# One decoder layer on one core: two steps at a time in every other period of the first attention

## The chip, the cores and the metric

The kernel runs on one core of a Trainium2 chip, in one launch. The metric is the device time of a launch in microseconds (us). The core has five engines that run side by side and wait for each other by semaphores only: TensorE (PE, with its weight loads PEld), VectorE (DVE), ScalarE (ACT), GpSimd (POOL) and SyncE (SP), which issues the DMAs. Each engine takes its own instructions in the order in which the program lists them.

## The reference, cut to what matters

```python
def attn(x, emb_weight, qkv_w, o_w):          # first attention: B 4, S 512, C 256, 16 heads of 64
    q, k, v = split_heads(x @ qkv_w.T)
    bias = emb_weight[rel_buckets(S)].transpose(2, 0, 1)[None]
    scores = einsum('bhqd,bhkd->bhqk', q, k) * 64 ** -0.5 + bias
    a = einsum('bhqk,bhkd->bhqd', softmax(scores), v)
    return merge_heads(a) @ o_w.T
x = layernorm(x + attn(x, ...))
x = layernorm(x + attn2(x, ctx, ...))         # 16 heads of 16: causal self part plus a context part
x = layernorm(experts(x, ...))                # 3 of 8 zones for each of the 4 sequences
```

Only the first attention is changed.

## The kernel before

`attention_1` works through 32 units. A unit u is a pair of heads (u % 8) of one sequence (u // 8). A software pipeline of 36 slots (`for t in range(SLOTS)`), each of four periods (`for i in range(NT)`), spreads a unit over five slots. In slot t these units are at work at the same time:

- unit t: projections. `proj_qk(t, 0)` (queries) and `proj_qk(t, 1)` (keys) are six float16 matmuls of 512 columns each (L409), `proj_v` 24 of 128 columns (L419). All three write `bank_a`. ACT (`evacuate` L610, `store_v` L616) and DVE (`low` L742) take the result out as a high and a low half in float16.
- unit t - 1: `maximum`, in each period two matmuls on half of the rows (L432) into `bank_m`, and on DVE two custom passes (L753) that give the row maximum of each of two heads for 128 queries, in `mx`.
- unit t - 2: `rows` in period 0: four transposes in float32 (L441) turn `mx` into rows of `bank_a`; ACT copies them twice with a scale into the two heads of `q2` (L623) and counts `act_rows`. Then the scores: in each period two (one for each head) of 128 keys by 512 queries, two matmuls each (L454, L455), into `bank_s[0]` and `bank_s[1]`. DVE adds the near bias (`add_bias` L762), ACT takes the exponential (L635). Scores 0 to 5 of a unit stand in periods 1, 2, 3 of slot u + 2, scores 6 and 7 in period 0 of slot u + 3. A score waits for the exponential of the score two before it, since it takes that bank.
- units t - 2 and t - 3: `pv` (L464), in each period the product of 128 keys with the values for both heads, in float32, two matmuls of 64 output rows (four records), added up in `bank_o` over four periods. POOL adds the exponentials up (`add_exponentials` L844) and makes a low half of the sums (L849). ACT and DVE take `bank_o` out in period 2 (`high_o` L648, `low_o` L767).
- unit t - 4: `sums` (L482) in period 0 turns the sums into a column of `bank_e[0]`, DVE inverts them (`invert` L774), and in each period `project_out` (L504) makes 128 tokens of the output product, three pairs of matmuls of 256 columns, one bank for each head. DVE adds the first head to `x_acc` (`add_out` L784), ACT scales the second (`weigh` L656), POOL adds that (L856).

The order on PE within a period is: first score, projection, second score, (period 0: `rows`, `sums`), `maximum`, `project_out`, `pv`. ACT and DVE follow the same order with their parts; in period 0 ACT does both exponentials, then the copies of `rows`, then `weigh`.

The waits that matter around the change are in `proj_qk`, for i == 0, and in `score`, for j == 0:

```python
if u > 1:
    pe.wait_ge(sm["act_rows"], 2 * u - 2)     # proj_qk(u, 0): bank_a is free of the rows of unit u - 2
...
    pe.wait_ge(sm["act_rows"], 2 * u + 2)     # score(u, 0): its own rows of maxima are in q2
```

`proj_qk(u, 1)` waits for `low` of the queries and `proj_v(u)` for `low` of the keys (`dve_a`), since all of them use `bank_a`.

Of the kernel before, what the change touches and what calls it, by code (L numbers as in the profile page):

```python
# [11 lines left out]
P = 128  # L12
# [197 lines left out]
def attention_1(nc, io, x_acc, xhi, xlo, ident, second, lines32, lines16, far_lines, halves2):  # L210
# [6 lines left out]
    with ExitStack() as ctx:  # L217
# [3 lines left out]
        def bank(n):  # L221
# [5 lines left out]
                                       "pool_lo pe_sum dve_r pe_o act_o dve_o pe_e0 pe_e1 dve_x act_x pool_x "  # L227
                                       "cst2 w2_in w2_hi w2_lo ld_ctx bias pe_br act_br dve_br dve_e1 dve_lo")
        moved = [sm[f"moved{c}"] for c in range(3)]
# [14 lines left out]
        junk = [sb(f"junk{p}", [P, S], F16) for p in range(2)]  # L244
        mx = [sb(f"mx{p}", [P, NT, 2]) for p in range(2)]
        pt = sb("pt", [P, RING, S])
        ps = [sb(f"ps{h}", [P, S]) for h in range(2)]
# [29 lines left out]
        def out_banks(u, qb):  # L277

            return bank_s if u >= LAST and qb % 2 == 1 else bank_e

# [9 lines left out]
        def sync(sp):  # L290
# [33 lines left out]
            for c in range(3):  # L324
                sp.dma_start(k2[c][D1:ROWS1, :, :], io["select1"]).then_inc(sm["cst"], DMA)
            for b in range(1, B):
                load_x(b)
                load_w(2 * b)
                load_w(2 * b + 1)
# [12 lines left out]
            for u in range(UNITS):  # L342
# [23 lines left out]
                if u == 4:  # L366
                    for dst, name in ((second.tri_q[:, :, :], "tri_q"), (second.identm[:, :, :], "identm"),
                                      (second.ident16[:, :], "ident16"), (second.braw[:, :], "b2")):
# [15 lines left out]
        def tensor(pe):  # L384
# [50 lines left out]
            def rows(u):  # L435
                pe.wait_ge(sm["dve_b"], 8 * u + 8)
                pe.wait_ge(sm["act_v"], min(u + 2, UNITS))
                if u == UNITS - 1:
                    pe.wait_ge(sm["act_rows"], 2 * u)
                for qb in range(NT):  # L440
                    mm = pe.transpose(bank_a[0:2, qb * P:(qb + 1) * P], mx[u % 2][:, qb, :], ident[:, :])  # L441
                mm.then_inc(sm["pe_rows"], 1)
# [25 lines left out]
            def sums(u):  # L468
                if u < UNITS - 1:
                    pe.wait_ge(sm["pool_lo"], 2 * u + 2)  # L470
                else:
                    pe.wait_ge(sm["dve_lo"], 2)
                if u == 0:
                    pe.wait_ge(sm["ones"], 1)
                    turned.done(pe)
                else:
                    pe.wait_ge(sm["dve_x"], 4 * u if u <= LAST else 4 * u - 1)
                for h in range(2):
                    for qb in range(NT):
                        for i in range(2):  # L480
                            n = h * NT + qb
                            mm = pe.matmul(bank_e[0][:, n:n + 1], psh[h][:, i, qb * P:(qb + 1) * P], ones[:, :], start=i == 0,  # L482
                                           stop=i == 1)
                mm.then_inc(sm["pe_sum"], 1)

            def project_out(u, qb):
                n = 4 * u + qb
                if qb == 0:
                    pe.wait_ge(sm["dve_o"], u + 1)
# [3 lines left out]
                if n == 4 * LAST + 1:  # L493
                    pe.wait_ge(sm["act_s"], 8 * UNITS)
                elif n > 4 * LAST + 1:
                    pe.wait_ge(sm["dve_e1"], n - 1 - 4 * LAST)
                elif n > 0:
                    pe.wait_ge(sm["dve_x"], n)
                    pe.wait_ge(sm["act_x"], n)
                tok = slice(qb * P, (qb + 1) * P)  # L500
                for n, (i, w) in enumerate(((0, wohi), (0, wolo), (1, wohi))):
                    for h in range(2):
                        hd = slice(h * D1, (h + 1) * D1)
                        mm = pe.matmul(out_banks(u, qb)[h][:, 0:C], a16[u % 2][hd, i, tok], w[hd, u % PAIRS, :], start=n == 0,  # L504
                                       stop=n == 2)
                        if n == 2:
                            mm.then_inc(sm[f"pe_e{h}"], 1)
# [29 lines left out]
            for t in range(SLOTS):  # L537
                for i in range(NT):
# [18 lines left out]
                    if 0 <= t - 1 < UNITS:  # L557
                        maximum(t - 1, i)
                    if 0 <= t - 4 < UNITS:
                        project_out(t - 4, i)  # L560
                    u = t - 2 if i > 1 else t - 3
                    if 0 <= u < UNITS:
                        pv(u, (i + 2) % 4)
                    for e in bridge_at(t, i):
                        bridge(e)

        def scalar(act):
# [82 lines left out]
            def weigh(u, qb):  # L650
                n = 4 * u + qb
                act.wait_ge(sm["pe_e1"], n + 1)
# [3 lines left out]
                act.activation(part[n % 4][:, :], bank_e[1][:, 0:C], ACT.Identity, scale=r[u % 2][:, 1, qb:qb + 1]  # L656
                               ).then_inc(sm["act_x"], 1)
# [39 lines left out]
        def vector(dve):  # L697
# [46 lines left out]
            def maximum(u, qb):  # L744
                if qb == 0 and u > 1:
                    dve.wait_ge(sm["pe_rows"], u - 1)
                if qb == 0:
                    dve.wait_ge(sm[f"rt{u % 3}"], DMA * (u // 3 + 1))
                for h in range(2):
# [26 lines left out]
            def add_out(u, qb):  # L776
                dve.wait_ge(sm["pe_e0"], 4 * u + qb + 1)
# [6 lines left out]
                dve.scalar_tensor_tensor(x_acc[:, o:o + C], out_banks(u, qb)[0][:, 0:C], r[u % 2][:, 0, qb:qb + 1], x_acc[:, o:o + C],  # L784
                                         ALU.mult, ALU.add).then_inc(sm["dve_x"], 1)
                if u >= LAST:
                    dve.wait_ge(sm["pe_e1"], 4 * u + qb + 1)
                    dve.wait_ge(sm["dve_x"], 4 * u + qb + 1)
                    dve.scalar_tensor_tensor(x_acc[:, o:o + C], out_banks(u, qb)[1][:, 0:C], r[u % 2][:, 1, qb:qb + 1], x_acc[:, o:o + C],
                                             ALU.mult, ALU.add).then_inc(sm["dve_e1"], 1)  # L790

            for t in range(SLOTS):
                for i in range(NT):
                    u = t - 2 if i > 0 else t - 3
                    if i == 2 and 0 <= t - 3 < UNITS:
                        low_o(t - 3)
# [16 lines left out]
                    if 0 <= t - 1 < UNITS:  # L813
                        maximum(t - 1, i)
                    if 0 <= t - 4 < UNITS:
                        add_out(t - 4, i)
                    if t in (6, 10) and i == 1:
                        split_w2(t // 10)
                    if t == 11 and i == 1:
                        dve.wait_ge(sm["cst2"], 4 * DMA)  # L820
                        dve.tensor_scalar(second.bias[:, :], second.braw[:, :], WS, None, ALU.mult).then_inc(sm["bias"], 1)
# [11 lines left out]
        def gpsimd(pool):  # L833
# [1162 lines left out]
```

## Time and profile before

| | |
|---|---|
| runs | 1284.3 us median of 3 (1284.05 to 1286.31) |
| profiled execution | 1287.09 us, of which 1285.4 us span |
| PE busy | 1183.4 us (92% of the span) |
| DVE busy | 924.5 us (72%) |
| ACT busy | 820.9 us (64%) |
| POOL busy | 498.6 us (39%) |
| granted TensorE clock, mean | 0.981 |

The profile is of one execution. Engine times are busy times; a PE record overlaps the next one, because matmuls are pipelined, so that the distance between two starts says what a matmul costs the queue. The first attention takes the span from the start to about 568 us. The chain of work that ended last runs over PE for 75% of the span, DVE 14%, ACT 4%.

### The profile page before, as it was taken

The numbers are of one execution on the slowest core, as the hardware profiler recorded it, in microseconds if no ns is written. First come the engines' busy times: TensorE is split into PE (matmuls) and PEld (weight loads), VectorE is DVE, ScalarE is ACT, GpSimd is POOL, SyncE is SP. The second block draws the span as 40 slices with busy tenths as digits, with TensorE's granted clock in tenths as the row PEclk, the third lists the DMA queues.
The fourth block names the chain that finished last, engine by engine and source line by source line (L and its number), as shares of the span: only waits on it lengthen the run. The fifth ranks groups of instructions, "written<-read, shape, count | busy, mean of one in ns | idle before, by whom it ended". The sixth has DMA issues, their size and how long they took to land.

```text
span 1285.4 us, 25128 instructions
## 1 busy us (share of the span) xinstructions
PE 1183.4 (92%) x8870; PEld 542.9 (42%) x8870; DVE 924.5 (72%) x2376; ACT 820.9 (64%) x1577; POOL 498.6 (39%) x519
## 2 busy tenths in 40 slices
PE   6799999999999999868899988888888999999998
PEld 2344444444444444334333233322332366666666
DVE  3777777777777777767788787778876567656564
ACT  3566666666666666634677766676666777667663
POOL 0167878888777778914212111131111131000000
PEclk9999999999999999988999999999999899999999
DMA  7634333322233332021121221122100523232300
GB/s 221 172 98 117 96 93 84 111 80 80 80 84 83 84 82 81 13 71 42 46 81 43 65 61 42 43 56 69 42 26 1 197 89 109 75 139 97 118 17 17
DMA packets 82483, 103.00 MB, mean 80 GB/s; under 512 B 12627, under 2 KB 74067, under 8 KB 82327
## 3 DMA queue, kind: packets, MB, share of 16 engines
q1 hardware_dynamic: 81174, 100.87, 26.8%
q8 instruction: 71, 1.16, 0.4%
q10 hardware_dynamic: 160, 0.39, 0.1%
q14 instruction: 54, 0.43, 0.1%
q0 software_dynamic: 1024, 0.13, 0.1%
HBM read 65.37 MB, written 10.68 MB: 59 GB/s over the span
## 4 chain that ended last, share of the span: by engine, by line
PE 75%; DVE 14%; ACT 4%; issue 4%; DMA 1%; POOL 1%; ACTq 0%; SPq 0%; DVEq 0%; POOLq 0%
PE a_s L1299 10%; PE a_o L464 9%; DVE a_mx L1607 8%; PE a_m L1285 7%; PE a_o L1218 6%; PE a_a L409 6%; PE a_s L454 5%; PE a_s L455 4%; PE a_m L1173 4%; PE a_e L504 3%; PE a_a L419 3%; PE a_m L432 3%; PE a_a L166 3%; PE a_s L1200 3%; PE a_s L1285 2%
## 5 line engine op out<-in xcount | busy, mean ns | idle before, releaser
L1607 DVE TENSOR_REDUCE a_mx<-a_m 128x1 f32<-128x512 f32 (+3 forms) x512 | 271.5, 583 | 80.4 <-PE a_m L1173 71.3
L1432 ACT ACTIVATE a_pt<-a_s 128x512 f32<-128x512 f32 (+3 forms) x512 | 235.0, 515 | 115.4 <-PE a_s L1200 112.9
L635 ACT ACTIVATE a_pt<-a_s 128x512 f32<-128x512 f32 x256 | 149.5, 597 | 167.4 <-DVE a_s L762 139.6
L753 DVE CUSTOM_DVE_ANT_0 a_junk<-a_m,a_rtile 128x512 f16<-128x512 f32 x256 | 167.3, 687 | 0.7 <-issue 0.7
L844 POOL TENSOR_TENSOR a_ps<-a_ps,a_pt 128x512 f32<-128x512 f32 x128 | 159.8, 1271 | 0.7 <-ACT a_pt L635 0.7
L464 PE MATMUL a_o<-a_pt,a_v 128*64 128x512 f32 x512 | 139.8, 624 | 2.6 <-DVE a_a L767 2.5
L1853 POOL TENSOR_SCALAR_AFFINE_SELECT a_pt<-a_pt 128x512 f32<-128x512 f32 x64 | 40.6, 635 | 229.4 <-ACT a_pt L1432 229.4
L762 DVE TENSOR_TENSOR a_s<-a_s,a_near 128x218 f32<-128x218 f32 (+1 forms) x256 | 107.9, 433 | 13.8 <-PE a_s L455 10.6
L454 PE MATMUL a_s<-a_q,a_k 128*128 128x512 f16 x256 | 99.3, 388 | 7.1 <-ACT a_pt L635 6.1
L742 DVE TENSOR_TENSOR a_nat<-a_a,a_nat 128x512 f16<-128x512 f32 x64 | 44.3, 692 | 84.2 <-ACT a_nat L610 84.2
L844 POOL TENSOR_TENSOR a_ps<-a_pt 128x512 f32<-128x512 f32 x64 | 80.1, 1273 | 57.0 <-ACT a_pt L635 57.0
L1173 PE MATMUL a_m<-a_qk 48*128 48x512 f16 (+3 forms) x320 | 78.4, 349 | 23.0 <-DVE a_mx L1607 22.6
L856 POOL TENSOR_TENSOR x_acc<-x_acc,a_part 128x256 f32<-128x256 f32 x120 | 87.2, 726 | 32.1 <-DVE x_acc L784 31.4
L455 PE MATMUL a_s<-a_q,a_k 74*128 74x512 f16 x256 | 98.2, 383 | 0.0
L849 POOL TENSOR_TENSOR a_psh<-a_ps,a_psh 128x512 f16<-128x512 f32 x62 | 70.5, 1157 | 68.0 <-ACT a_psh L641 67.9
L1218 PE MATMUL a_o<-a_pt,a_vy 128*17 128x512 f32 (+3 forms) x768 | 86.6, 523 | 0.0
L1734 DVE SCALAR_TENSOR_TENSOR x_acc<-a_s,a_wbc,x_acc 128x256 f32<-128x256 f32 x48 | 23.2, 484 | 85.8 <-PE a_s L1299 85.6
L454 PEld LDWEIGHTS a_s<-a_q,a_k 128*128 128x128 f16 x256 | 24.8, 97 | 131.1 <-issue 70.5
L1496 ACT ACTIVATE a_held<-a_m 128x512 f32<-128x512 f32 x72 | 43.0, 597 | 57.9 <-PE a_m L1285 57.1
L1200 PE MATMUL a_s<-a_qk 49*128 49x512 f16 (+3 forms) x320 | 70.4, 342 | 2.0 <-ACT a_pt L1432 1.9
L1173 PEld LDWEIGHTS a_m<-a_qk 48*128 48x128 f16 x320 | 22.4, 93 | 113.9 <-DVE a_mx L1607 86.4
L504 PE MATMUL a_e<-a_wohi,a_a 64*128 64x256 f16 x496 | 61.7, 271 | 5.3 <-issue 4.6
(295 smaller groups left out, 2622.8 us busy)
## 6 DMA issues: line engine op xcount, KB each, us to landing
a_rtile<-lines SPq DMA_DIRECT2D x32, 448.0 KB, 3.9
a_q<-a_nat SPq DMA_DIRECT2D x192, 64.0 KB
a_k<-a_nat SPq DMA_DIRECT2D x192, 64.0 KB
a_vy<-in_Wa SPq DMA_DIRECT2D x12, 1024.0 KB, 4.9
a_vy<-in_Wb SPq DMA_DIRECT2D x12, 1024.0 KB, 7.4
a_qk<-halves SPq DMA_DIRECT2D x40, 128.0 KB, 2.7
halves<-a_held SPq DMA_DIRECT2D x16, 256.0 KB, 2.3
halves<-a_held SPq DMA_DIRECT2D x32, 128.0 KB, 2.4
```

The source lines that it names most:

```text
L454: pe.matmul(bank_s[h][:, :], k1[c][:, h, ks], q1[c][:, h, ::-1], start=True, stop=False)
L455: pe.matmul(bank_s[h][:, :], k2[c][:, h, ks], q2[c][:, h, ::-1], start=False, stop=True).then_inc(sm["pe_s"], 1)
L464: mm = pe.matmul(bank_o[h * D1:(h + 1) * D1, :], v[u % 3][:, kb, h * D1:(h + 1) * D1], pt[:, (8 * u + 2 * kb + h) % RING, :], start=kb == ...
L635: act.activation(pt[:, n % RING, ::-1], bank_s[j % 2][:, :], ACT.Exp, scale=SC1 / QS).then_inc(sm["act_s"], 1)
L753: dve.tensor_tensor_reduce(junk[h][:, :], bank_m[h][:, :], rtile[:, u % 3, h, qb * P:qb * P + S], 1.0, -3e38, ALU.add, ALU.max, mx[u % 2][ ...
L844: pool.tensor_tensor(ps[h][:, :], pt[:, (8 * u + h) % RING, :] if kb == 1 else ps[h][:, :], pt[:, (8 * u + 2 * kb + h) % RING, :], ALU.add ...
L1173: mm[h] = pe.matmul(bank_m[j % 3][:, 0:keys], q[u % 3][o:o + ROW_M, pair, x, qb * P:(qb + 1) * P], k[u % 3][o:o + ROW_M, pair, x, 0:keys], ...
L1218: mm = pe.matmul(bank_o[h * 2 * D2:h * 2 * D2 + D2 + 1, first:], v[u // GROUPS][:, x * NT + kb, u % GROUPS * G2 + h, :], pt[g % 4][:, h, f ...
L1285: mm = pe.matmul(up[f % 4][:, :], w[c3][:, c * FF + f * P:c * FF + (f + 1) * P], m[:, c, b * S:(b + 1) * S], start=i == 0, stop=i == len(s ...
L1299: mm = pe.matmul(down[t], a[u % 2][:, f, tok], w[c3][:, HALF + f * C:HALF + (f + 1) * C], start=i == 0, stop=i == len(steps) - 1)
L1432: act.activation(pt[g % 4][:, h, first:], bank_s[(32 * u + j) % 3][:, first:], ACT.Exp, scale=SC2 / QS).then_inc(sm["act_s"], 1)
L1607: dve.tensor_reduce(mx[u % 2][:, qb, to:to + 1], bank_m[j % 3][:, 0:keys], AX.X, ALU.max).then_inc(sm["dve_b"], 1)
```

## The change

- In periods 1 and 3 PE does two `project_out` and two `pv` in a row, in periods 0 and 2 none. `weigh` and `add_out` on ACT, DVE and POOL follow in pairs, each unit's two blocks in the two halves of one bank instead of one after the other in the same columns.
- `high_o` and `low_o` move from period 2 to period 3.
- `proj_qk(t, 0)` moves from between the two scores of period 1 to the end of period 0, behind `rows`, `sums` and `maximum`.
- `rows`: DVE first scales the maxima and writes them in float16 (`negative`, a new instruction of 8 columns, at the end of `maximum` in period 3), and PE turns them by four float16 matmuls with a float16 identity, which is loaded at the start. The scale leaves ACT's copies.

The diff, cut to its core:

```diff
         def out_banks(u, qb):
-            return bank_s if u >= LAST and qb % 2 == 1 else bank_e
+            half = slice(qb % 2 * C, (qb % 2 + 1) * C)
+            return [bank[:, half] for bank in (bank_s if u >= LAST and qb >= 2 else bank_e)]
...
# sync
                 sp.dma_start(k2[c][D1:ROWS1, :, :], io["select1"]).then_inc(sm["cst"], DMA)
+            sp.dma_start(second.ident16[:, :], io["ident16"]).then_inc(sm["ld_id16"], DMA)
...
# tensor
             def rows(u):
-                pe.wait_ge(sm["dve_b"], 8 * u + 8)
+                pe.wait_ge(sm["dve_n"], u + 1)
                 pe.wait_ge(sm["act_v"], min(u + 2, UNITS))
...
-                    mm = pe.transpose(bank_a[0:2, qb * P:(qb + 1) * P], mx[u % 2][:, qb, :], ident[:, :])
+                    mm = pe.matmul(bank_a[0:2, qb * P:(qb + 1) * P], mx16[:, qb, :], second.ident16[:, :], start=True, stop=True)
...
             def project_out(u, qb):
...
-                elif n > 0:
+                elif n > 0 and n % 2 == 0:
                     pe.wait_ge(sm["dve_x"], n)
                     pe.wait_ge(sm["act_x"], n)
...
                     if t < UNITS:
-                        if i == 1:
-                            proj_qk(t, 0)
                         if i == 2:
                             proj_qk(t, 1)
...
                     if 0 <= t - 1 < UNITS:
                         maximum(t - 1, i)
-                    if 0 <= t - 4 < UNITS:
+                    if i == 0 and t < UNITS:
+                        proj_qk(t, 0)
+                    if i % 2 == 1 and 0 <= t - 4 < UNITS:
+                        project_out(t - 4, i - 1)
                         project_out(t - 4, i)
-                    u = t - 2 if i > 1 else t - 3
-                    if 0 <= u < UNITS:
-                        pv(u, (i + 2) % 4)
+                    u = t - 2 if i == 3 else t - 3
+                    if i % 2 == 1 and 0 <= u < UNITS:
+                        pv(u, (i + 1) % 4)
+                        pv(u, (i + 1) % 4 + 1)
...
# scalar
-                    act.activation(q2[u % 3][D1:D1 + 2, h, :], bank_a[0:2, :], ACT.Copy, scale=-1 / MAXROW
+                    act.activation(q2[u % 3][D1:D1 + 2, h, :], bank_a[0:2, :], ACT.Copy
                                    ).then_inc(sm["act_rows"], 1)
...
-                    if i == 2 and 0 <= t - 3 < UNITS:
+                    if i == 3 and 0 <= t - 3 < UNITS:
                         high_o(t - 3)
...
-                    if 0 <= t - 4 < LAST:
+                    if i % 2 == 1 and 0 <= t - 4 < LAST:
+                        weigh(t - 4, i - 1)
                         weigh(t - 4, i)
...
# vector
+            def negative(u):
+                dve.wait_ge(sm["dve_b"], 8 * u + 8)
+                if u > 0:
+                    dve.wait_ge(sm["pe_rows"], u)
+                dve.tensor_scalar(mx16[:, :, :], mx[u % 2][:, :, :], -1 / MAXROW, None, ALU.mult).then_inc(sm["dve_n"], 1)
...
-                    if i == 2 and 0 <= t - 3 < UNITS:
+                    if i == 3 and 0 <= t - 3 < UNITS:
                         low_o(t - 3)
...
                     if 0 <= t - 1 < UNITS:
                         maximum(t - 1, i)
-                    if 0 <= t - 4 < UNITS:
+                        if i == NT - 1:
+                            negative(t - 1)
+                    if i % 2 == 1 and 0 <= t - 4 < UNITS:
+                        add_out(t - 4, i - 1)
                         add_out(t - 4, i)
...
# gpsimd
-                    if 0 <= u < LAST:
-                        add_out(u, (i + 3) % 4)
+                    if i % 2 == 0 and 0 <= u < LAST:
+                        add_out(u, (i + 2) % 4)
+                        add_out(u, (i + 2) % 4 + 1)
```

## Rows read from the trace of the kernel before

**Rows 1.** Stretches: us, busy of PE, PEld, DVE, ACT, POOL, clock, DMA.
```profile
77.55:517.42 439.87, 435.40 (x3361) 186.13 (x3360) 334.92 (x1124) 290.03 (x562) 347.78 (x336) 1.00 0.33 91
...
545.30:548.71 3.41, 3.41 (x14) 0.57 (x10) 1.82 (x5) 1.48 (x2) 3.41 (x4) 0.50 0.01 2
```

**Rows 2.** Timeline (start, duration, instruction), transposes of slots 4, 24 and 32.
```profile
77.55 0.60 PE L441 MATMUL a_a<-ident,a_mx 128*2 128x128 f32 x4
...
393.07 0.60 PE L441 MATMUL a_a<-ident,a_mx 128*2 128x128 f32 x4
...
517.42 0.60 PE L441 MATMUL a_a<-ident,a_mx 128*2 128x128 f32 x4
```

**Rows 3.** Timeline of PE, from period 3 of slot 24 to period 1 of slot 25.
```profile
404.15 0.22 PE L419 MATMUL a_a<-a_whi,xhi 128*128 128x128 f16 x1
...
405.49 0.38 PE L454 MATMUL a_s<-a_q,a_k 128*128 128x512 f16 x1
...
406.02 0.39 PE L432 MATMUL a_m<-a_nat 64*128 64x512 f16 x2
406.24 0.27 PE L504 MATMUL a_e<-a_wohi,a_a 64*128 64x256 f16 x2
...
406.67 1.08 PE L464 MATMUL a_o<-a_pt,a_v 128*64 128x512 f32 x4
407.68 0.39 PE L454 MATMUL a_s<-a_q,a_k 128*128 128x512 f16 x1
...
408.17 0.39 PE L454 MATMUL a_s<-a_q,a_k 128*128 128x512 f16 x1
...
408.62 0.60 PE L441 MATMUL a_a<-ident,a_mx 128*2 128x128 f32 x4
409.05 0.54 PE L482 MATMUL a_e<-a_ones,a_psh 128*128 128x1 f16 x16
409.53 0.39 PE L432 MATMUL a_m<-a_nat 64*128 64x512 f16 x2
409.94 0.28 PE L504 MATMUL a_e<-a_wohi,a_a 64*128 64x256 f16 x2
...
410.38 1.08 PE L464 MATMUL a_o<-a_pt,a_v 128*64 128x512 f32 x4
411.39 0.39 PE L454 MATMUL a_s<-a_q,a_k 128*128 128x512 f16 x1
...
411.83 0.38 PE L409 MATMUL a_a<-xhi,a_whi 128*128 128x512 f16 x1
...
413.13 0.38 PE L454 MATMUL a_s<-a_q,a_k 128*128 128x512 f16 x1
```

**Rows 4.** Timeline of ACT in the same slots.
```profile
402.70 0.59 ACT L610 ACTIVATE a_nat<-a_a 128x512 f16<-128x512 f32 x1
...
408.85 1.09 ACT L635 ACTIVATE a_pt<-a_s 128x512 f32<-128x512 f32 x2 [0.38 <-DVE a_s L762]
409.96 1.06 ACT L623 ACTIVATE a_q<-a_a 2x512 f16<-2x512 f32 x2
```

**Rows 5.** Timeline of PE in slot 2, which has no `project_out` and no `pv`.
```profile
44.40 0.39 PE L432 MATMUL a_m<-a_nat 64*128 64x512 f16 x2
45.66 0.38 PE L454 MATMUL a_s<-a_q,a_k 128*128 128x512 f16 x1 [0.87 <-issue]
```

**Rows 6.** Timeline of DVE in slots 24 and 25.
```profile
403.32 0.69 DVE L742 TENSOR_TENSOR a_nat<-a_a,a_nat 128x512 f16<-128x512 f32 x1 [1.23 <-ACT a_nat L610]
403.93 0.48 DVE L762 TENSOR_TENSOR a_s<-a_s,a_near 128x308 f32<-128x308 f32 x1
404.32 0.69 DVE L753 CUSTOM_DVE_ANT_0 a_junk<-a_m,a_rtile 128x512 f16<-128x512 f32 x1
...
405.55 0.48 DVE L784 SCALAR_TENSOR_TENSOR x_acc<-a_e,a_r,x_acc 128x256 f32<-128x256 f32 x1
...
408.35 0.86 DVE L762 TENSOR_TENSOR a_s<-a_s,a_near 128x218 f32<-128x218 f32 x2
```

More of the change, by code:

```diff
@@ L227, in attention_1 @@
                                        "pool_lo pe_sum dve_r pe_o act_o dve_o pe_e0 pe_e1 dve_x act_x pool_x "
-                                       "cst2 w2_in w2_hi w2_lo ld_ctx bias pe_br act_br dve_br dve_e1 dve_lo")
+                                       "cst2 w2_in w2_hi w2_lo ld_ctx bias pe_br act_br dve_br dve_e1 dve_lo dve_n ld_id16")
         moved = [sm[f"moved{c}"] for c in range(3)]
@@ L245, in attention_1 @@
         mx = [sb(f"mx{p}", [P, NT, 2]) for p in range(2)]
+        mx16 = sb("mx16", [P, NT, 2], F16)
         pt = sb("pt", [P, RING, S])
@@ L366, in sync @@
                 if u == 4:
-                    for dst, name in ((second.tri_q[:, :, :], "tri_q"), (second.identm[:, :, :], "identm"),
-                                      (second.ident16[:, :], "ident16"), (second.braw[:, :], "b2")):
+                    for dst, name in ((second.tri_q[:, :, :], "tri_q"), (second.identm[:, :, :], "identm"), (second.braw[:, :], "b2")):
                         sp.dma_start(dst, io[name]).then_inc(sm["cst2"], DMA)
@@ L439, in rows @@
                     pe.wait_ge(sm["act_rows"], 2 * u)
+                if u == 0:
+                    pe.wait_ge(sm["ld_id16"], DMA)
                 for qb in range(NT):
-                    mm = pe.transpose(bank_a[0:2, qb * P:(qb + 1) * P], mx[u % 2][:, qb, :], ident[:, :])
+                    mm = pe.matmul(bank_a[0:2, qb * P:(qb + 1) * P], mx16[:, qb, :], second.ident16[:, :], start=True, stop=True)
                 mm.then_inc(sm["pe_rows"], 1)
@@ L476, in sums @@
                 else:
-                    pe.wait_ge(sm["dve_x"], 4 * u if u <= LAST else 4 * u - 1)
+                    pe.wait_ge(sm["dve_x"], 4 * u if u <= LAST else 4 * u - 2)
                 for h in range(2):
@@ L492, in project_out @@
                     pe.wait_ge(sm["dve_r"], u + 1)
-                if n == 4 * LAST + 1:
+                if n == 4 * LAST + 2:
                     pe.wait_ge(sm["act_s"], 8 * UNITS)
-                elif n > 4 * LAST + 1:
-                    pe.wait_ge(sm["dve_e1"], n - 1 - 4 * LAST)
-                elif n > 0:
+                elif n > 4 * LAST + 2 and n % 2 == 0:
+                    pe.wait_ge(sm["dve_e1"], n - 2 - 4 * LAST)
+                elif n > 0 and n % 2 == 0:
                     pe.wait_ge(sm["dve_x"], n)
@@ L503, in project_out @@
                         hd = slice(h * D1, (h + 1) * D1)
-                        mm = pe.matmul(out_banks(u, qb)[h][:, 0:C], a16[u % 2][hd, i, tok], w[hd, u % PAIRS, :], start=n == 0,
+                        mm = pe.matmul(out_banks(u, qb)[h], a16[u % 2][hd, i, tok], w[hd, u % PAIRS, :], start=n == 0,
                                        stop=n == 2)
@@ L651, in weigh @@
                 n = 4 * u + qb
-                act.wait_ge(sm["pe_e1"], n + 1)
+                act.wait_ge(sm["pe_e1"], n // 2 * 2 + 2)
                 act.wait_ge(sm["dve_r"], u + 1)
@@ L655, in weigh @@
                     act.wait_ge(sm["pool_x"], n - 3)
-                act.activation(part[n % 4][:, :], bank_e[1][:, 0:C], ACT.Identity, scale=r[u % 2][:, 1, qb:qb + 1]
+                act.activation(part[n % 4][:, :], out_banks(u, qb)[1], ACT.Identity, scale=r[u % 2][:, 1, qb:qb + 1]
                                ).then_inc(sm["act_x"], 1)
@@ L745, in maximum @@
                 if qb == 0 and u > 1:
-                    dve.wait_ge(sm["pe_rows"], u - 1)
+                    dve.wait_ge(sm["dve_n"], u - 1)
                 if qb == 0:
@@ L776, in add_out @@
             def add_out(u, qb):
-                dve.wait_ge(sm["pe_e0"], 4 * u + qb + 1)
+                dve.wait_ge(sm["pe_e0"], 4 * u + qb // 2 * 2 + 2)
                 dve.wait_ge(sm["dve_r"], u + 1)
@@ L783, in add_out @@
                 o = (u // PAIRS * NT + qb) * C
-                dve.scalar_tensor_tensor(x_acc[:, o:o + C], out_banks(u, qb)[0][:, 0:C], r[u % 2][:, 0, qb:qb + 1], x_acc[:, o:o + C],
+                dve.scalar_tensor_tensor(x_acc[:, o:o + C], out_banks(u, qb)[0], r[u % 2][:, 0, qb:qb + 1], x_acc[:, o:o + C],
                                          ALU.mult, ALU.add).then_inc(sm["dve_x"], 1)
                 if u >= LAST:
-                    dve.wait_ge(sm["pe_e1"], 4 * u + qb + 1)
+                    dve.wait_ge(sm["pe_e1"], 4 * u + qb // 2 * 2 + 2)
                     dve.wait_ge(sm["dve_x"], 4 * u + qb + 1)
-                    dve.scalar_tensor_tensor(x_acc[:, o:o + C], out_banks(u, qb)[1][:, 0:C], r[u % 2][:, 1, qb:qb + 1], x_acc[:, o:o + C],
+                    dve.scalar_tensor_tensor(x_acc[:, o:o + C], out_banks(u, qb)[1], r[u % 2][:, 1, qb:qb + 1], x_acc[:, o:o + C],
                                              ALU.mult, ALU.add).then_inc(sm["dve_e1"], 1)
@@ L819, in vector @@
                     if t == 11 and i == 1:
-                        dve.wait_ge(sm["cst2"], 4 * DMA)
+                        dve.wait_ge(sm["cst2"], 3 * DMA)
                         dve.tensor_scalar(second.bias[:, :], second.braw[:, :], WS, None, ALU.mult).then_inc(sm["bias"], 1)
```

## Prediction

> **What bounds the kernel now.** I read the stretches first. In slots 4 to 31 of the first attention, 77.55 to 517.42 us, PE is busy 435.4 of 439.9 us at full clock, and no other engine above 80% [rows 1]. The transposes of successive slots give the pace: 28 slots in 439.87 us, 20 of them in 315.52 us. Two of the 28 also split weights of the second attention and are about 2.15 us longer, so a plain slot takes (439.87 - 4.5) / 28 = 15.54 us [rows 2]. The timeline of PE then shows no long gap in a slot, so PE's queue sets the pace; but this holds because each wait for ACT or DVE has just enough PE work in front of it, and the change moves that work. The reader should follow period 0 [rows 3, 4], because everything is decided there.
>
> **What PE saves.** From starts in [rows 3]:
> - Switches. A second score costs 0.44 us, but 0.53 if `maximum` follows (405.49 to 406.02): 0.1 us to go from the full array to half its rows. `project_out` costs 0.11 a pair, 0.33 us, but 0.43 before `pv` (406.24 to 406.67). `pv` costs 1.01 us (406.67 to 407.68) where its four passes of 512 columns, at the 0.216 us that such a column count costs (six in the 1.30 us from 411.83 to 413.13), would cost 0.86: 0.15 for leaving. Before, each of four periods pays all three. After, periods 1 and 3 pay all three and periods 0 and 2 pay one in and one out (0.1 each), so a slot saves 2 x (0.10 + 0.15 - 0.10) = 0.3 us. The unknown is the second of two `pv`: 0.86 if it follows without a gap, 1.01 if not; I take 0.86, as nothing changes between them. Then 0.3, at worst 0.
> - `rows`: four float32 transposes take 0.43 us (408.62 to 409.05). Float16 matmuls of 128 columns cost 0.056 (24 in the 1.34 us from 404.15 to 405.49), so 0.22: 0.21 saved, between 0 and 0.21.
> - `project_out` of period 0 waited for the inverted sums: `maximum` to `project_out` is 0.41 there (409.53 to 409.94) and 0.22 in period 3. It now comes a period later: 0.19 saved.
> - Score 7 waited for the exponential of score 5: 0.49 from 407.68 to 408.17, else 0.44. 0.05 saved.
>
> Together 0.75 us of a slot; PE's own need is about 14.8 us. The new DVE scaling has eight columns; I bound it between nothing and a full 128 x 512 pass (0.69, [rows 6]). It ends over 1 us before PE wants the rows (below), so it costs nothing. The identity is one more DMA in SP's queue at the start, in front of the loads of x[1..3]: 0 to 0.6 us, once. The halves of one bank in place of one area, and POOL's pairs, add no instruction. POOL is busy 347.8 of 439.9 us [rows 1], 12.4 us a slot, and its next queued sums still end before ACT wants them, since ACT does so only in period 2.
>
> The Trainium skill ("TensorEngine Tiling (Array Packing)", section Key Properties) says that changing the tiling mode, not just the tile, drains TensorE. By that rule alone two switches fewer a slot are a gain and the change is faster; the trace agrees with the rule, with 0.1 to 0.15 us a switch [rows 3].
>
> **First wait: the projection of queries for `bank_a`.** Call the start of score 6 in period 0 T0 (407.68). DVE starts on it at +0.67, ACT at +1.17 (408.85), both exponentials end at +2.26, and ACT's two copies of the rows run from +2.28 (409.96) to +3.34 [rows 4, 6]. This chain starts with PE's own score and has no slack in it. Before, PE filled the time with transposes, sums, `maximum`, `project_out` and `pv` until +3.71 (411.39), and the next score, which needs the same rows, found them ready. After the change `project_out` and `pv` are gone from period 0: scores 0.88, `rows` 0.22, sums 0.48, `maximum` with switch 0.32, so PE reaches `proj_qk(t, 0)` at T0 + 1.90. It writes `bank_a`, which holds the rows until ACT has copied them, so it starts at about +3.43 (0.08 for the semaphore). PE stands for 1.53 us, and queued behind it is everything. That this wait is real shows in slot 2, which has neither `project_out` nor `pv`: there the score stands 0.87 us idle, from `maximum` at 44.40 to 45.66, and ACT had no exponentials ahead of the copies in that slot [rows 5]. Period 0 then ends at T0 + 3.43 + 1.30 = +4.73, against +3.71 before.
>
> **Second wait: `proj_v` for DVE.** Let 0 be the start of score 0 in period 1. DVE gaps from starts in [rows 6]: a 512-column half 0.61 (403.32 to 403.93), a bias addition 0.39 (0.3 for the narrow one), a pair of maxima 1.23 (404.32 to 405.55), an addition to `x_acc` 0.40. ACT: exponential to next 0.49, evacuation 0.59 long [rows 4]. Bias 0.67, exponential 1.17, evacuation of queries 1.66 to 2.25 (its projection is already there), low half 2.28, bias of score 1 at 2.89, two maxima 3.2 to 4.42, now two additions to `x_acc` to 5.22, and only then the bias of score 2, to 5.70. Exponential 5.81, evacuation of keys 6.30 to 6.89, low half to 7.61, so `proj_v` can start at 7.7.
> PE: period 1 is 0.44 + 0.53 + 0.22 + 0.66 + 0.10 + 0.86 + 1.01 = 3.82, period 2 is 0.44 + 1.30 + 0.53 + 0.32 = 2.59, and score 4 0.44: PE is there at 6.85. It stands 0.86 us. Before, the second `project_out` and `pv` of periods 1 and 2 stood in front of `proj_v`, and it came at 8.3 (404.15, against 411.39 less a slot of 15.54, 395.85 [rows 3]). The cover is gone here too.
>
> **The new slot.** 7.71 + `proj_v` 1.34 + score 5 0.53 + `maximum` 0.22 + outputs 0.66 + 0.10 + `pv` 1.87 = 12.43 at T0; + 3.43 + 1.30 = 17.16 us. DVE's scaling ends near 12.0 and is wanted at 13.3; `low_o` ends near 9.9 and `pv` wants it at 10.6. So a slot is 17.16 - 15.54 = 1.62 us longer: 2.39 us of waits less 0.77 saved. 28 slots: 45.4 us. Slots 32 and 33 keep the rows' wait and get the same heavy period 1 and 3; I take 1.6 each, 3.2. Slot 3 and the end (the last two outputs now stand behind the bridge's last step on DVE, 2 x 2 additions of 0.48 in place of two): 3 us, between 0 and 5. Sum +51.6.
>
> From the profiled execution, 1287.09 us, this gives 1338.7. That execution is 2.8 us above the median of the runs, 1284.3, so on the median 1336.
>
> **Rivals.**
> 1. Only the first wait. If DVE and ACT run a little earlier than in my chain, `proj_v` isn't late: 14.78 + 1.53 = 16.31, +0.77 a slot, 28 slots 21.6 us, with the ends 26: 1310. For it: the second wait is a difference of two long sums, and an error of 0.3 in either moves it. Against it: each term of the chain has a row.
> 2. The clock falls. Period 0 now holds `rows`, sums of one column and 1.5 us of nothing. At 545.3 us, after such a stretch in the pipeline's end, the granted clock is 0.50 (1.2 of 2.4 GHz) for 3.4 us [rows 1], which costs 1.7 us of work. In a third to two thirds of the slots, with half of it absorbed by waits: 28 x 0.5 x 1.7 x 0.6 = 14 us more, 1350, and up to 1384 if every slot paid it in full. Against it: slot 2 with its idle stretch ran at full clock. The Trainium skill ("TensorE: Matmul & The Clock Gate", section What's actually happening) says that the gate follows how busy TensorE has been; here only the rows above show it.
> 3. Faster. If the projection isn't held up, PE's 14.78 us rule: 28 x -0.76 = -21, and 1263. It decides if ACT's copies end before T0 + 1.9 and DVE's low half 0.9 us earlier. For it: PE is the fullest engine and it saves 0.75 us. Against: the chain from score 6 to the copies takes 3.34 us by rows, and nothing in the change shortens it but the scale of a copy. If only half of each wait appears it is a tie.
>
> **How the numbers follow.** Forecast 1336: 0.62, own range 1326 to 1346 (switches 0 to 0.3 and the second wait 0.6 to 0.95 over 28 slots). Only the first wait 0.15, clock falls 0.14, faster 0.07, tie 0.02. The range from 1306 to 1356 takes in the forecast, most of rival 1 and the nearer half of rival 2. A measurement of this kernel tells about 0.2% from no change. Slower by more 0.91, within 0.02, faster 0.07.
>
> **What would show it.** Right: transposes 17.2 us apart; a gap of PE of 1.5 us before the first L409 of a slot, put down to ACT's copy (`a_q`); one of 0.8 before the first `proj_v` matmul, put down to DVE; PE's share of the stretch down to some 86%; `rows` in 0.22. Wrong: the first gap under 0.5 us would mean that the copies come earlier than I chained them; a slot under 16 us that the second doesn't appear; half-clock stretches inside the pipeline, rival 2.

## The result and the profile after

The changed kernel takes 1344.8 us (median of 4 runs, 1339.9 to 1345.2) against 1285.3 us for the kernel before in the same runs: a ratio of 1.046, with a 95% interval from 1.043 to 1.050. The profiled execution took 1345.1 us. The page's first part, after the change:

```profile
span 1343.4 us, 25131 instructions
PE 1182.5 (88%) x8870; PEld 550.8 (41%) x8870; DVE 937.0 (70%) x2408; ACT 814.5 (61%) x1577; POOL 498.3 (37%) x519
```

PE has the same busy time as before (1183.4) in a span 58 us longer: it did not get more work, it stood still longer. The same view as [rows 1] shows where; the columns are the stretch, its length, busy time and count of PE, PEld, DVE, ACT, POOL, granted clock, DMA share and GB/s:

```profile
80.81:571.68 490.87, 434.17 (x3361) 191.08 (x3361) 346.80 (x1152) 284.44 (x562) 346.98 (x335) 0.98 0.30 81
246.82:554.60 307.78, 274.00 (x2162) 120.57 (x2162) 220.05 (x739) 181.10 (x360) 224.03 (x217) 1.00 0.29 79
116.16:138.23 22.07, 18.09 (x122) 8.26 (x121) 14.26 (x43) 11.44 (x21) 13.66 (x15) 0.85 0.39 100
189.68:210.87 21.19, 16.85 (x122) 7.94 (x122) 14.19 (x43) 11.33 (x21) 13.07 (x14) 0.92 0.28 79
```

The first is slots 4 to 31, 490.87 us where it was 439.87 [rows 1, 2]: +51.0. The second is slots 13 to 30 at full clock, PE busy for 89%. The third and fourth are slots 6 and 10, the two that split weights of the second attention.

The timeline of PE from the transposes of slot 23 to the first projection of slot 24, to read beside [rows 3] (start, duration, instruction, idle time in brackets):

```profile
417.65 0.38 PE L445 MATMUL a_a<-a_ident,a_mx 128*2 128x128 f16 x4
...
421.38 0.38 PE L458 MATMUL a_s<-a_q,a_k 128*128 128x512 f16 x1
...
423.33 1.94 PE L468 MATMUL a_o<-a_pt,a_v 128*64 128x512 f32 x8
425.20 0.39 PE L458 MATMUL a_s<-a_q,a_k 128*128 128x512 f16 x1
...
427.47 0.39 PE L434 MATMUL a_m<-a_nat 64*128 64x512 f16 x2
427.82 0.39 PE L458 MATMUL a_s<-a_q,a_k 128*128 128x512 f16 x1
...
429.03 0.23 PE L421 MATMUL a_a<-a_whi,xhi 128*128 128x128 f16 x1 [0.61 <-DVE a_nat L749]
...
433.76 0.39 PE L458 MATMUL a_s<-a_q,a_k 128*128 128x512 f16 x1
...
434.20 0.38 PE L458 MATMUL a_s<-a_q,a_k 128*128 128x512 f16 x1
...
434.73 0.39 PE L445 MATMUL a_a<-a_ident,a_mx 128*2 128x128 f16 x4
435.05 0.55 PE L486 MATMUL a_e<-a_ones,a_psh 128*128 128x1 f16 x16
435.53 0.39 PE L434 MATMUL a_m<-a_nat 64*128 64x512 f16 x2
437.18 0.38 PE L411 MATMUL a_a<-xhi,a_whi 128*128 128x512 f16 x1 [1.26 <-issue]
```

A slot is 434.73 - 417.65 = 17.08 us. There are two gaps that were not there before: 0.61 before the first `proj_v` matmul, put down to DVE's low half, and 1.26 before the first projection of the queries, which the view labels "issue". What it waits for stands on ACT, in the same slot:

```profile
434.91 1.09 ACT L641 ACTIVATE a_pt<-a_s 128x512 f32<-128x512 f32 x2 [0.82 <-DVE a_s L775]
436.02 1.06 ACT L629 ACTIVATE a_q<-a_a 2x512 f16<-2x512 f32 x2
```

The copies of the rows end at 437.08, PE starts at 437.18. From score 6 (433.76) that is +3.42. The same chain in [rows 4] was as long, but then PE had work until +3.71. In slot 32, which has no projection, the same gap stands before score 0, and there the view names ACT's copies as the releaser:

```profile
574.13 0.38 PE L458 MATMUL a_s<-a_q,a_k 128*128 128x512 f16 x1 [1.26 <-ACT a_q L629]
```

### The profile page after: what moved, and what is told of

Same layout as the page of the kernel before. It is cut to its first block, busy times and chain, and to the rows that moved or that the text cites. A ratio compares the mean times of both kernels' runs of the same rounds, so it can differ in the third digit from the quotient of the medians.

```text
span 1343.4 us, 25131 instructions
## 1 busy us (share of the span) xinstructions
PE 1182.5 (88%) x8870; PEld 550.8 (41%) x8870; DVE 937.0 (70%) x2408; ACT 814.5 (61%) x1577; POOL 498.3 (37%) x519
## 4 chain that ended last, share of the span: by engine, by line
PE 60%; DVE 20%; issue 11%; ACT 7%; DMA 1%; ACTq 0%; SPq 0%; DVEq 0%
PE a_s L1316 9%; DVE a_mx L1624 8%; PE a_m L1302 7%; PE a_o L1235 6%; PE a_o L468 5%; PE a_m L1190 4%; PE a_a L411 4%; PE a_a L421 3%; DVE a_s L775 3%; ACT a_nat L616 3%; PE a_s L1217 3%; PE a_a L166 3%; PE a_s L458 2%; PE a_s L459 2%; PE a_s L1302 2%
## 5 line engine op out<-in xcount | busy, mean ns | idle before, releaser
L468 PE MATMUL a_o<-a_pt,a_v 128*64 128x512 f32 x512 | 126.0, 613 | 0.1
L411 PE MATMUL a_a<-xhi,a_whi 128*128 128x512 f16 x128 | 49.3, 385 | 40.0 <-issue 37.8
L1190 PE MATMUL a_m<-a_held 48*128 48x128 f16 (+3 forms) x192 | 48.1, 355 | 19.5 <-DVE a_mx L1624 18.0
```

Source lines behind the costliest of these rows:

```text
L468: mm = pe.matmul(bank_o[h * D1:(h + 1) * D1, :], v[u % 3][:, kb, h * D1:(h + 1) * D1], pt[:, (8 * u + 2 * kb + h) % RING, :], start=kb == ...
L1190: mm[h] = pe.matmul(bank_m[j % 3][:, 0:keys], q[u % 3][o:o + ROW_M, pair, x, qb * P:(qb + 1) * P], k[u % 3][o:o + ROW_M, pair, x, 0:keys], ...
```

## The experiments

My theory was the two waits: period 0 has lost the cover for ACT's copies (the work that PE does while the copies are made), and DVE's chain to `proj_v` has lost its own. A rival was that the move of the projection alone did the harm; another, that the pairs cost something by themselves; a third, that the granted clock is the cause. The third is out for most of the stretch: slots 13 to 30 are 1.54 us longer at full clock.

### The projection back in its place

```diff
+                        if i == 1:
+                            proj_qk(t, 0)
...
-                    if i == 0 and t < UNITS:
-                        proj_qk(t, 0)
```

> The changed kernel with one part undone: proj_qk(t, 0) stands between the scores of period 1 again, all pairs stay. Theory (what holds PE in period 0 is the missing cover for ACT's copies of the rows, whoever waits for them): score 0 of period 1 waits for the same copies, so PE still stands until 3.42 us after score 6; but the evacuation chain starts earlier against PE and proj_v is no longer late, so a slot falls from 17.08 to about 16.3 us and the kernel to about 1322 us. Rival (moving the projection in front of the copies is itself the cause of the first wait): the wait goes too, a slot is near 15.0 us, the kernel near 1287 us.

Measured: 1335.2 us, ratio 1.038 (1.034 to 1.041). In the trace the slots are 16.56 us and every third or fourth 18.25 us. The two stretches between successive `rows`, and the wait:

```profile
393.17:409.73 16.56, 15.18 (x121) 6.70 (x120) 12.32 (x42) 10.28 (x20) 12.44 (x13) 1.00 0.28 82
409.73:427.98 18.25, 16.88 (x122) 7.14 (x121) 12.34 (x42) 10.28 (x20) 12.45 (x13) 0.91 0.26 67
```
```profile
427.00 0.39 PE L458 MATMUL a_s<-a_q,a_k 128*128 128x512 f16 x1
...
430.43 0.38 PE L458 MATMUL a_s<-a_q,a_k 128*128 128x512 f16 x1 [1.26 <-ACT a_q L629]
```

The first wait is unchanged, +3.43 us after score 6 and now named: whoever comes next waits. So the move isn't its cause; the rival falls. The second wait shrinks to 0.3 us. The plain slot is 0.5 us shorter, not 0.8, and in every third or fourth slot the granted clock fell to half for a while (the mean of that slot is 0.91), which costs 1.7 us there. Slots 13 to 30 take 17.12 us each on average against 17.10: in these slots the clock took back what the shorter second wait had given. That the kernel is still 10 us faster than the changed one comes from elsewhere: the two slots that split weights take 18.6 us each, where they took 22.1 and 21.2, and slot 4 begins 3 us earlier.

### ACT's copies between the two exponentials

```diff
+                    if i == 0 and 0 <= t - 2 < UNITS:
+                        rows(t - 2)
                     if 0 <= u < UNITS:
                         exponential(u, (i + 3) % 4 * 2 + 1)
-                    if i == 0 and 0 <= t - 2 < UNITS:
-                        rows(t - 2)
```

> The changed kernel with ACT's two copies of the rows between the exponentials of scores 6 and 7 instead of behind both. Theory (the first wait is ACT's queue): the copies end about 0.5 us earlier, the first projection starts at 2.9 us instead of 3.42 after score 6, a slot is 16.55 us, the kernel about 1330 us. Rival (PE waits there for something else, such as DVE's inverted sums or maxima): no change, 1344 us.

Measured: 1328.6 us, ratio 1.033 (1.030 to 1.037).

```profile
435.67 0.39 PE L458 MATMUL a_s<-a_q,a_k 128*128 128x512 f16 x1
...
438.61 0.38 PE L411 MATMUL a_a<-xhi,a_whi 128*128 128x512 f16 x1 [0.77 <-issue]
```

The projection starts 2.94 us after score 6, the gap falls by 0.49 and the slot from 17.08 to 16.59 (420.06 to 436.65 between transposes). So what PE waits for there is the copies in ACT's queue, and not DVE's sums or maxima. The 0.77 us that are left come from the rest of the chain: the bias, one exponential and the copies themselves.

### DVE's additions behind the next bias

```diff
                     if 0 <= u < UNITS:
                         add_bias(u, (i + 3) % 4 * 2)
+                    if i == 2 and 0 <= t - 4 < UNITS:
+                        add_out(t - 4, 0)
+                        add_out(t - 4, 1)
...
-                    if i % 2 == 1 and 0 <= t - 4 < UNITS:
-                        add_out(t - 4, i - 1)
-                        add_out(t - 4, i)
+                    if i == 3 and 0 <= t - 4 < UNITS:
+                        add_out(t - 4, 2)
+                        add_out(t - 4, 3)
```

> The changed kernel with DVE's additions of blocks 0 and 1 to x_acc behind the bias of score 2 in period 2, where DVE stands idle, instead of ahead of it. Theory (the second wait is DVE's chain bias - exponential - evacuation - low half): proj_v starts 0.5 us earlier against score 0, 0.3 us of wait stay, a slot is 16.6 us, the kernel about 1331 us. Rival (the second wait follows the first, DVE is not its cause): no change, 1344 us.

Measured: 1346.8 us, ratio 1.048 (1.045 to 1.052), which reads like the rival. The trace says otherwise. Its slots:

```profile
414.15:430.71 16.56, 15.18 (x121) 6.68 (x120) 12.28 (x42) 10.18 (x20) 12.44 (x13) 1.00 0.30 84
430.71:448.89 18.18, 16.80 (x122) 7.07 (x121) 12.31 (x42) 10.18 (x20) 12.46 (x13) 0.91 0.25 67
```

At full clock the slot is 16.56 us, half a microsecond shorter, just as expected: `proj_v` follows score 4 (424.29) with 0.3 us of wait, at 425.03. But in every third or fourth slot the clock falls at the end of the first wait, as the distances of starts below show (0.42 us from one 512-column matmul to the next, where it is 0.22 elsewhere):

```profile
433.17 0.58 PE L411 MATMUL a_a<-xhi,a_whi 128*128 128x512 f16 x1 [1.26 <-issue]
...
435.68 0.63 PE L458 MATMUL a_s<-a_q,a_k 128*128 128x512 f16 x1
436.10 0.55 PE L459 MATMUL a_s<-a_q,a_k 74*128 74x512 f16 x1
```

Slots 13 to 30 take 17.03 us each on average, against 17.10 in the changed kernel. In these slots a gain of 0.5 us was real and was paid back by the clock. Over slots 4 to 31 the run is 5 us ahead (485.83 us), since its slots with the splits are shorter. It loses that again in front of slot 4 (1.6 us) and between slot 32 and the second attention (57.0 us where it was 51.5), and why it does there stays open.

### All three at once

Edit: the three diffs above together.

> The changed kernel with all three edits at once: projection back in period 1, copies early, additions to x_acc later. Theory: score 0 of period 1 starts 2.9 us after score 6, proj_v no longer waits, a slot is 15.8 us, 0.26 us more than before the change, the kernel about 1293 us. If the granted clock also falls in a third of the slots, as it did with either edit alone, 1.7 us each, about 1308 us. Rival (the pairs cost something of their own beside the two waits): a slot above 16.3 us, the kernel above 1310 us with the clock up.

Measured: 1310.2 us, ratio 1.019 (1.015 to 1.024). The clock stayed up (1.00 from 250 to 530 us, PE busy 95%), and the slot is 16.08 us, not 15.8; that is below the 16.3 of the rival. The total near 1308 us is luck: that figure took the clock to fall in a third of the slots, and it did not.

```profile
428.69 0.38 PE L458 MATMUL a_s<-a_q,a_k 128*128 128x512 f16 x1
...
429.54 0.39 PE L458 MATMUL a_s<-a_q,a_k 128*128 128x512 f16 x1
...
430.26 0.23 PE L421 MATMUL a_a<-a_whi,xhi 128*128 128x128 f16 x1
```
```profile
429.52 0.69 DVE L749 TENSOR_TENSOR a_nat<-a_a,a_nat 128x512 f16<-128x512 f32 x1 [0.66 <-ACT a_nat L616]
```

Score 4 (429.54) ends its turn at 429.98, `proj_v` starts at 430.26: 0.28 us of wait remain, in this kernel as in the two before. It is a third loop that I had not seen: from the end of `proj_qk(t, 1)` (428.69) `bank_a` needs 1.57 us to go through ACT and DVE before `proj_v` may write it, and between them stand only a score, `maximum` and a score, 1.29 us. Before the change `project_out` and `pv` of period 2 stood there too. With 0.77 us left of the first wait, 1.05 us of waits remain, less the 0.53 us that PE saves (below): that gives 0.52 of the 0.54 us by which the slot is longer than before. Over 28 slots this makes 15 of the 23 us between the two spans. The other 8 us lie behind slot 32, and no run was made for them. In no run are both waits gone.

### Pairs in periods 0 and 2

```diff
+                    if i == 0 and 0 <= t - 3 < UNITS:
+                        pv(t - 3, 0)
+                        pv(t - 3, 1)
+                    if i % 2 == 0 and 0 <= t - 4 < UNITS:
+                        project_out(t - 4, i)
+                        project_out(t - 4, i + 1)
+                    if i == 2 and 0 <= t - 3 < UNITS:
+                        pv(t - 3, 2)
+                        pv(t - 3, 3)
```

`weigh` and `add_out` stand in the same periods, `high_o` and `low_o` late in period 3, `proj_qk(t, 0)` in period 1.

> The changed kernel with its pairs of project_out and pv in periods 0 and 2 instead of 1 and 3 (pv by unit u in slot u + 3 only), the projection of the queries in period 1, the evacuation of bank_o late in period 3. The switches saved stay, but the pairs stand behind rows, where ACT's copies need cover. Theory: PE reaches score 0 of period 1 at 4.7 us after score 6, later than the copies at 3.4, no first wait; proj_qk(t, 1) waits 0.3 us for DVE; a slot is about 15.4 us, the kernel 1282 us, between 1278 and 1295. Rival (pairs in every other period are bad wherever they stand, since DVE and ACT are fed unevenly): a slot over 16 us, the kernel over 1300 us.

Measured: 1417.8 us, ratio 1.101 (1.096 to 1.106). My sum was wrong by 136 us, and what the rival said of the numbers came true. The plain slots are 18.13 us long at full clock and up to 20.7 with the lower one, the mean clock from 250 to 560 us is 0.88. Two rows of DVE and PE, the first from a slot at full clock:

```profile
467.04 0.88 DVE L799 SCALAR_TENSOR_TENSOR x_acc<-a_e,a_r,x_acc 128x256 f32<-128x256 f32 x2 [1.14 <-PE a_e L508]
```
```profile
442.64 0.59 PE L445 MATMUL a_a<-a_ident,a_mx 128*2 128x128 f16 x4 [1.61 <-DVE a_mx L769]
```

The pair covers ACT's copies, and score 0 follows without a gap. But DVE's two additions now stand in its queue in period 0 and wait for the outputs, which come last in PE's period: 1.1 us at full clock, 2.8 to 3.2 in most slots with a stretch at the lower clock, where PE itself is later. In every slot `rows` waits 1.6 us for DVE's scaled maxima. I had followed PE's chain but had not written down DVE's; that the wait in period 0 is what makes DVE late in period 3 is my reading of the order, and no run tests it. That the pairs were the right thing in the wrong period is refuted in this form; a form that gives DVE other work there wasn't tried.

### The splits moved

```diff
-                    if t in (6, 10) and i == 1:
+                    if t in (6, 10) and i == 0:
```

> The changed kernel with the two splits of the second attention's weights (ACT 1.3 us, DVE 1.6 us, in slots 6 and 10) moved from the end of period 1 to the end of period 0, where both engines stand idle. Theory: those two slots are 22.1 and 21.1 us long against 17.1 because the split stands in the chain to proj_v; moved, they fall to about 18, the kernel falls by 7 us to 1338 us. Rival (their excess is only the fallen clock): no change, 1344 us.

Measured: 1339.8 us, ratio 1.041 (1.037 to 1.045). Between the transposes of slots 6 and 7:

```profile
116.71 0.39 PE L445 MATMUL a_a<-a_ident,a_mx 128*2 128x128 f16 x4
...
135.16 0.38 PE L445 MATMUL a_a<-a_ident,a_mx 128*2 128x128 f16 x4
```

That slot is 18.45 us where it was 22.07, as expected, and slot 10 has the same length. The kernel is 5 us faster by the medians and 7 by the ratios, with intervals that just overlap. The rival, that the excess was only the fallen clock, is not the whole: in the run with early copies slot 6 ran at full clock and was 19.19 us against 16.60. So some 2.6 us are the chain, and the clock adds to it in the changed kernel, where PE stood for 2.54 us up to 128.92 and the granted clock was at half from 128.41 on (0.85 in that slot). My reading is that a chain which is already late by 0.8 us takes every further step in full.

### The float16 rows alone, in the kernel before

Edit: `negative`, `mx16`, the float16 matmuls and the early identity, nothing else.

> The kernel before with the float16 rows alone (scaling on DVE, float16 matmuls, identity loaded at the start). By the prediction's term, 0.21 us a slot: 1279 us. By the trace of the changed kernel, where the step from the last score to sums takes 0.85 us against 0.88 before because a 0.1 us gap now stands on either side of the matmuls: 0.03 us a slot, 1284 us, no change.

Measured: ratio 1.002 (1.000 to 1.004), a slot of 15.53 us (394.52 to 410.05 between transposes). No gain that the runs can tell: the prediction's 0.21 us isn't there.

### The same with 128 columns

```diff
-        mx16 = sb("mx16", [P, NT, 2], F16)
+        mx16 = sb("mx16", [P, NT, P], F16)
...
-                    mm = pe.matmul(bank_a[0:2, qb * P:(qb + 1) * P], mx16[:, qb, :], second.ident16[:, :], start=True, stop=True)
+                    mm = pe.matmul(bank_a[:, qb * P:(qb + 1) * P], mx16[:, qb, :], second.ident16[:, :], start=True, stop=True)
```

> The kernel before with float16 rows whose stationary side is 128 columns wide (the maxima in columns 0 and 1, zeros behind them) instead of 2. Theory (the gaps of 0.1 us on either side of the narrow float16 matmuls are changes of the tiling mode): the gaps go, from the last score to sums 0.66 us instead of 0.88, a slot is 15.33 us, the kernel 0.5% faster, ratio 0.995. Rival (the gaps come with the float16 matmuls for another reason, such as their loads of weights): 0.85 us stay, ratio 1.000.

Measured: ratio 1.002 (1.000 to 1.004), and both answers are right in part.

```profile
393.58 0.39 PE L458 MATMUL a_s<-a_q,a_k 128*128 128x512 f16 x1
...
394.31 0.38 PE L459 MATMUL a_s<-a_q,a_k 74*128 74x512 f16 x1
394.53 0.39 PE L445 MATMUL a_a<-a_ident,a_mx 128*128 128x128 f16 x4
394.75 0.54 PE L486 MATMUL a_e<-a_ones,a_psh 128*128 128x1 f16 x16
...
396.08 1.08 PE L468 MATMUL a_o<-a_pt,a_v 128*64 128x512 f32 x4
397.27 0.38 PE L458 MATMUL a_s<-a_q,a_k 128*128 128x512 f16 x1
```
```profile
393.99 0.17 DVE L765 TENSOR_SCALAR a_mx<-a_mx 128x8 f16<-128x8 f32 x1
394.10 0.48 DVE L795 SCALAR_TENSOR_TENSOR x_acc<-a_e,a_r,x_acc 128x256 f32<-128x256 f32 x1
394.50 0.67 DVE L773 TENSOR_TENSOR a_s<-a_s,a_near 128x218 f32<-128x218 f32 x2
```
```profile
396.11 1.06 ACT L627 ACTIVATE a_q<-a_a 2x512 f16<-2x512 f32 x2
```

The gaps are gone: `rows` takes 0.22 us in all, so they came with the two columns. The Trainium skill ("TensorEngine Tiling (Array Packing)", section Key Properties) says that a change of the tiling mode drains TensorE. The gaps fit that if two columns count as another mode, but no run separates it from a second reading, that of the loads of weights. Beside the narrow matmuls of the changed kernel the first load comes only with its matmul (434.73), beside the wide ones 0.22 us ahead of it:

```profile
434.73 0.20 PEld L445 LDWEIGHTS a_a<-a_ident,a_mx 128*2 128x2 f16 x4 [0.43 <-issue]
```
```profile
394.31 0.43 PEld L445 LDWEIGHTS a_a<-a_ident,a_mx 128*128 128x128 f16 x4
```

But a slot is still 15.50 us, because `pv` to score 0 is now 1.19 us, not 1.01. DVE's new scaling pushes its bias for score 6 to 0.92 us after score 6 (393.58), from 0.67 [rows 6]. ACT's copies end that much later (397.17), and PE, which would have been at score 0 by 397.09, waits for them until 397.27. In the kernel before this chain had about 0.3 us of slack; the two small edits used it up.

### pv ahead of project_out in period 0

```diff
+                    if i == 0 and 0 <= u < UNITS:
+                        pv(u, (i + 2) % 4)
                     if 0 <= t - 4 < UNITS:
                         project_out(t - 4, i)
-                    if 0 <= u < UNITS:
+                    if i > 0 and 0 <= u < UNITS:
                         pv(u, (i + 2) % 4)
```

and ACT's copies between the exponentials, in the kernel before.

> The kernel before with two small edits: in period 0 pv stands ahead of project_out, so that DVE's inversion of the sums is hidden, and ACT's copies of the rows stand between the exponentials of scores 6 and 7, so that they stay covered. Theory: the 0.19 us that project_out waits in period 0 go, a slot is 15.35 us, the kernel 0.4% faster, 1280 us. Rival (the switches in the new order cost what the wait did): 1285 us, no change.

Measured: ratio 1.000 (0.998 to 1.002); a slot is 15.45 us (389.96 to 405.41), 0.09 less. The wait of 0.19 is gone, but `maximum` in front of `pv` costs 0.32 us (406.32 to 406.64) where it cost 0.22 in front of `project_out`, and `project_out` still costs 0.43 (407.65 to 408.08): a switch more at `maximum` takes half back. The rival was half right, and 0.09 us a slot is below what the runs can tell.

### Wide rows, pv first, copies early

> The kernel before with the wide float16 rows, pv ahead of project_out in period 0, and ACT's copies between the two exponentials. Theory: 0.22 and 0.09 us a slot add up, a slot is 15.24 us, the kernel 0.7% faster than before, ratio 0.993. Rival (with less PE work in period 0 another wait, for the copies or for DVE, takes the place): a slot above 15.33, ratio above 0.995.

Measured: 1280.9 us, ratio 0.994 (0.992 to 0.997), faster than both kernels.

```profile
388.97 0.39 PE L445 MATMUL a_a<-a_ident,a_mx 128*128 128x128 f16 x4
...
404.20 0.39 PE L445 MATMUL a_a<-a_ident,a_mx 128*128 128x128 f16 x4
```

A plain slot is 15.23 us, to the hundredth what was expected. The wide rows alone gave 0.04 us and these two edits 0.09; together they give 0.31, since the early copies take away the wait into which the rows' gain had gone. But slots 4 to 31 are only 4.4 us shorter in all (435.45 against 439.87), half of 28 x 0.31. Four of them (5, 12, 19 and 28) are 0.8 us longer than the others, and the slot behind each of these 0.25. There DVE's scaling of eight columns takes 1.30 us instead of 0.17, and PE waits for it:

```profile
106.40 1.30 DVE L767 TENSOR_SCALAR a_mx<-a_mx 128x8 f16<-128x8 f32 x1
```
```profile
106.42 1.26 POOL L859 TENSOR_TENSOR a_ps<-a_pt 128x512 f32<-128x512 f32 x1
```
```profile
107.76 0.40 PE L445 MATMUL a_a<-a_ident,a_mx 128*128 128x128 f16 x4 [0.66 <-DVE a_mx L767]
```

In each of the four it lies beside an addition of POOL and ends 0.02 to 0.03 us after it. So the price of the new instruction isn't fixed by its eight columns; the two other runs with float16 rows in the kernel before have one and two such slots. That is the rival's other wait, in four slots of 28.

## Why the prediction was right

The direction, the mechanism and the size held: +51.6 us was forecast, +59.5 measured between medians, +58.0 between spans. The errors of the parts go both ways: the plain slots cost some 2 us less than forecast, the slots with the splits and the falling clock 8 us more, and 3.3 us came from the code behind the attention, for which the sum had no term. Step by step:

- The first wait: start of the projection at +3.43 us after score 6 forecast, +3.42 measured. Its length is 1.30 us (PE was ready at 435.88), not 1.53, because PE came later than I had it. The run with early copies shows the cause, the run with the projection put back shows that it is the lost cover and not the move.
- The second wait: `proj_v` at +7.71 after score 0 forecast, +7.65 measured (421.38 to 429.03). Its length is 0.77 us (PE was ready at 428.26), forecast 0.86. Moving DVE's additions behind the next bias took it to 0.3 us, which shows that they stood in its chain.
- The slot: 17.16 forecast, 17.08 measured.
- What PE saves: 0.77 forecast. Measured 17.08 - 1.30 - 0.77 = 15.01 of own need, so 0.53. The term that was wrong is the rows' 0.21 us: I took the price of float16 matmuls from 128-column ones, and with two columns a gap of 0.1 stands before and after. From the last score to sums it is 0.85 us against 0.88 before; 0.03 saved. The run of the rows alone confirms it. The pair of `pv` costs 1.87 us, as taken; `maximum` to a score 0.35, not 0.32.
- That the DVE scaling is free: true in the changed kernel (it ends 1.1 us before the transposes). It is not in the kernel before, where it delays a bias by 0.25 us and, beside an addition of POOL, takes up to 1.3 us, more than my upper bound of 0.69.
- The plain slots gave less and others more. Slots 4 to 31 were to cost 45.4 us and cost 51.0. At 1.54 us the plain slots alone would make 43.1. The term that was too small is the two slots that split weights, 5.0 and 4.1 us above a plain slot where I had left 2.15; the clock falling in slots 4 and 11 adds 2.9. Moving the splits took 5 to 7 us off.
- Slots 32, 33, the start and the end: 6.2 us forecast; measured +3.3 before slot 4 (80.81 against 77.55) and +0.5 behind slot 32, since the memset that opens the second attention stands at 623.13 against 568.39. The other 3.3 us of the 58 lie behind it, in code that isn't changed, where 44.4 us are at the lower clock and 34.1 were before. What brings them there wasn't tried.
- The rival that only the first wait counts is out, the second has its row. The faster one is out by both. The falling clock, at 0.14, is not what the changed kernel's plain slots show (full clock from slot 13 to 30), but its sign, stretches at half clock inside the pipeline, was there in slots 4, 6, 10 and 11, and two variants with shorter slots had it in every third or fourth slot. The argument against it was thin. Slot 2 of the kernel before ran at full clock, but only up to 60.61 us, right behind its longest gap; there the granted clock is 0.50 for 3.41 us:

```profile
59.16 0.39 PE L454 MATMUL a_s<-a_q,a_k 128*128 128x512 f16 x1 [2.97 <-ACT a_pt L635]
```

- Two more signs came out otherwise than written down: PE's share of the stretch is 88%, not some 86%, and the first gap is labelled "issue" in the slots with a projection; it is the view of slot 32 and the first two runs that put it down to ACT.

## What to carry to other kernels

Work that an in-order engine does between a producer and a wait is cover, also where it is slow by itself: before moving it, write down the round trip (here score, bias, exponential, copies: 3.4 us) and what is left in front of the wait. Do that for each engine that the moved step stands on; the run that did so for PE alone was off by 136 us. And two small gains that use the same slack don't add up, until the step that eats the slack is moved as well.

## What the runs showed of the hardware

- Four float16 matmuls with 2 stationary columns between matmuls with 128 columns had a gap of 0.1 us before and after them (434.42 to 434.73 and 434.73 to 435.05, where 0.22 each would do); with 128 columns, most of them zeros, they had none. The float32 transposes that they replaced had no such gap, though their shape has two columns too, at 0.107 us for 128 columns (0.43 for four, [rows 3]).
- Switches between full array, half rows and half columns cost 0.1 to 0.15 us each [rows 3]. The change was to save 0.3 us a slot of them; 0.26 is what is left of the measured 0.53 when the other terms (0.03, 0.19 and 0.05) are taken off, and that was small beside the waits.
- The granted clock fell to half (1.2 GHz) behind gaps of only 1.3 us, in every third or fourth slot of 16.56 us. It did not in the changed kernel's slots 12 to 31 of 17.08 us with the same gap, and not in slots 12 to 31 of 16.08 and 16.59 us with a gap of 0.77. So a shorter slot can be no faster. What decides it stays open; no run was made for it.
- DVE's scaling of 128 x 8 float32 to float16 took 0.17 us in most slots of the last run, 0.27 in most of the changed kernel, and 1.30 us in four slots of the last run. Wherever it took more than 0.17 us in these two traces, it ended 0.02 to 0.03 us after an addition on POOL. But in most slots of the last run an addition also began 0.01 to 0.02 us behind the scaling and didn't lengthen it; what decides between the two isn't shown.
